# Attention heads of a fused two-layer kernel: the division moved ahead of a round's first marking, and each exponential placed two slots behind its turned scores

## The reference, cut to what matters

```
qr, kr = apply_rope(q, cos, sin), apply_rope(k, cos, sin)
draft = einsum('bhqd,bhkd->bhqk', qr, kr) + causal(neg)
_, draft_indices = top_k(draft, 128)
mask = full(neg); mask[draft_indices] = 0; mask = causal(neg)
attn = softmax(draft / 4 + mask)
out = einsum('bhqk,bhkd->bhqd', attn, v) @ Wo.T
```

## Time and profile before

| | |
|---|---|
| median of the runs | 3397.38 us |
| the profiled execution | 3398.37 us |
| its span | 3396.6 us |
| TensorE matmul, busy | 3019.7 us (89%) |
| VectorE, busy | 2404.0 us (71%) |
| ScalarE, busy | 1961.9 us (58%) |
| GpSimd, busy | 1532.1 us (45%) |
| attention heads, from the first sample to the last division | 2115.5 to 3256.2 us |

### The profile page before, as it was taken

The page is one execution under the profiler, slowest core; times in us unless marked ns, Lnnn a source line. Parts: engine busy times, 40 slices in busy tenths (PEclk is TensorE's granted clock), DMA queues, the critical chain, the costliest instruction groups (busy, mean ns, idle before and its releaser), DMA issues. The chain is left out here.

```text
span 3396.6 us, 49801 instructions
## 1 busy us (share of the span) xinstructions
PE 3019.7 (89%) x15644; PEld 1834.0 (54%) x15737; DVE 2404.0 (71%) x4659; ACT 1961.9 (58%) x4170; POOL 1532.1 (45%) x3508
## 2 busy tenths in 40 slices
PE   7999999999999999999999877487888788888779
PEld 4455454554554645545445435266666666666654
DVE  5677696786876967769679428587777777777640
ACT  1464564545545635456455115788888888888621
POOL 2245263362442633625426200766666666666410
PEclk9999999999999999999999988577777777777889
DMA  2222132231322322313212010000000000000010
GB/s 83 62 84 84 70 116 81 69 106 68 97 72 79 115 74 81 91 71 106 87 53 97 13 45 1 1 1 1 1 2 1 2 2 1 1 2 1 1 48 25
DMA packets 65800, 169.58 MB, mean 50 GB/s; under 512 B 11776, under 2 KB 19328, under 8 KB 64512
## 3 DMA queue, kind: packets, MB, share of 16 engines
q1 hardware_dynamic: 54448, 115.17, 10.5%
q10 hardware_dynamic: 11088, 51.19, 4.3%
HBM read 161.08 MB, written 5.24 MB: 49 GB/s over the span
## 5 line engine op out<-in xcount | busy, mean ns | idle before, releaser
L1898 ACT ACTIVATE X<-ah_z,ah_trial 128x256 bf16<-128x256 f32 (+6 forms) x896 | 732.4, 824 | 25.0 <-POOL ah_trial L2001 13.9
L1082 ACT ACTIVATE m_mix<-m_mix,m_cs 128x128 f32<-128x128 f32 x1024 | 312.9, 388 | 257.2 <-DMA m_mix<-cs_rows 257.2
L1853 PE MATMUL ah_ps_o<-a_v,X 128*128 128x17 f32 x2304 | 353.3, 282 | 44.8 <-DVE hT L2098 44.8
L1853 PEld LDWEIGHTS ah_ps_o<-a_v,X 128*128 128x128 f32 x2304 | 337.9, 220 | 52.1 <-ACT X L1909 49.7
L1909 ACT ACTIVATE X<-ah_ps_e 128x512 f32<-128x512 f32 (+3 forms) x384 | 185.8, 485 | 191.5 <-PE ah_ps_e L1840 128.5
L2070 DVE TENSOR_SCALAR_CACHE_REDUCE X<-ah_z,ah_cut 128x256 bf16<-128x256 f32 (+6 forms) x224 | 193.6, 875 | 128.7 <-POOL ah_cut L2006 128.7
L964 POOL TENSOR_TENSOR m_xdec<-m_xdt,m_decay_out 128x512 f32<-128x512 f32 x112 | 142.8, 1275 | 213.1 <-DVE m_xdt L1208 202.0
L887 PE MATMUL m_ps_x<-m_w_out,m_gate 128*128 128x512 f32 x512 | 234.1, 600 | 0.0
L887 PE MATMUL m_ps_d<-m_w_out,m_gate 128*128 128x512 f32 x512 | 233.5, 599 | 0.0
L2083 DVE MAX8 ah_top<-ah_ps_m 128x8 f32<-128x256 f32 (+6 forms) x224 | 185.9, 830 | 67.0 <-PE ah_ps_m L1803 58.8
L992 POOL TENSOR_TENSOR m_squares<-m_squares 128x256 f32<-128x256 f32 x128 | 104.1, 813 | 276.9 <-ACT m_squares L1094 276.9
(11 more groups left out here) (297 smaller groups left out, 7518.9 us busy)
## 6 DMA issues: line engine op xcount, KB each, us to landing
m_mix<-cs_rows SPq DMA_DIRECT2D x128, 512.0 KB, 4.5
m_w_proj<-in_w_proj ACTq DMA_DIRECT2D x69, 512.0 KB, 3.3
m_fade<-fade_rows SPq DMA_DIRECT2D x224, 128.0 KB, 3.0
m_w_out<-in_w_out ACTq DMA_DIRECT2D x7, 2048.0 KB, 7.7
X<-in_x SPq DMA_DIRECT2D x8, 256.0 KB, 5.0
m_w_out<-in_w_out SPq DMA_DIRECT2D x1, 2048.0 KB, 10.6
x_away<-X SPq DMA_DIRECT2D x1, 2048.0 KB, 10.9
X<-x_away SPq DMA_DIRECT2D x8, 256.0 KB, 7.3
```

What stands on the lines that cost most here:

```text
L1082: act.activation(mix[:, u % 3, h, :], mix[:, u % 3, h, :], ACT.Relu, bias=cs[:, c, h0 + h:h0 + h + 1], scale=-1.0).then_inc(lag_done, 1)
L1853: last = pe.matmul(ps_o[:, t, :], eT[:, g % 3, b * P:(b + 1) * P], v[:, b0 + b, h // REP, :], start=i == 0 and b == 0, stop=b0 + b == t, s ...
L1898: act.activation(sign[:, at % 2, 0:(t + 1) * P], z[:, h % RING, cols(t)], ACT.Sign, bias=trial[:, h % RING, 0, t - 1:t], scale=-1.0, accum ...
```

## The change

Two edits, both inside `attention_heads_fast`. `LATER` goes from 1 to 2, so slot `i` of ScalarE's round now holds chunk `i-2` of head n-3: slots 0 and 1 hold the last two chunks of head n-4, and slots 2 to 11 the first ten of head n-3. And VectorE's `divide(n - 4)` moves from behind pick 1, evacuation 1 and take 3 to a place ahead of take 1. TensorE's and GpSimd's lists stay as they are.

```
-    LATER = 1
+    LATER = 2
...
                     add_sample(n + 1)
+                if live(n - 4):
+                    divide(n - 4)
                 if live(n - 2):
                     take(n - 2, 1)
                     take(n - 2, 2)
...
-                    if t == 1 and live(n - 4):
-                        divide(n - 4)
```

## The result

The changed kernel takes 3390.3 us (median of 15 executions, fastest 3385.4), the kernel before 3396.3 on the same chips. The ratio is 0.998 [0.9972, 0.9988]: a real gain, of some 6 us and not of 38. One of the fifteen executions took 11779 us, with a mean granted clock of 0.57, and is left out of the ratio. The profiled execution took 3390.3 us with a span of 3388.5, which is 8.1 less than that of the profiled execution before. This is the rival "the two edits cancel", which I had given 14%.

A forecast was written before the change was run, and what follows sets the result against it. A ring of waits, no engine, bounds the kernel. Period 26.2 + 6.8 = 33.0 us, 1.12 less than 34.12, over 26 periods 29 us; 29 - 0.5 + 10 = 38, from 3398.4 to 3360 us, range 3318 to 3392.

The forecast's parts named there:

- the two edits cancel: Rival, 14%: late chunk 11 holds the division, which holds the marking; period stays 34.0 to 34.2 us, total say 3392.
- The ring: Chain of waits in the heads: marking, turned scores, exponential, last count, cut, next marking; 34.12 us a period.
- two new gates: Row copy waits for the twelfth chunk, 0.5 to 2 us; division, ahead of marking, waits for chunk 11's addition, some 3.
- The division moved: VectorE's division ahead of the first marking: TensorE's marked scores of tile 2 start 1.7 us earlier after it.
- The exponentials moved: ScalarE's exponentials get a slot of slack, on average 2.4 us; its 190 us of waits for turned scores largely go.
- X: Stretch from VectorE's first marking to the end of the twelfth chunk of turned scores: 26.2 us, between 25.05 and 26.9.
- the tail: Chain from ScalarE's row copy through chunk 11's exponential, its addition and the division to the next marking: 6.8 us, 6.2 to 7.4.
- three signs: Wrong if marking still waits for cut, twelfth chunk ends later than 27.3 us, or row copy to marking outside 6.2 to 7.4.
- Theory A: Links of the ring add up; making any link shorter or longer moves the period by as much.
- Theory B: Clock falls in step with rounds hold the period, 34.1 us; TensorE at another clock level offsets a changed link.
- The last rounds: Final periods of the heads, without new scores, less work on ScalarE: together about 10 us gained, between 4 and 13.
- The slower rival: Rival, 15%: low clock spreads to TensorE's stretch from chunk 8 to chunk 11; period 36.4 us, total 3450, milder 3423.

The follow-up runs named there:

- the pads: Changed kernel plus an unused VectorE reduction between division and first marking of each head: 384 columns (about 0.5 us), 3391.4 us; 1024 columns (1.2 us), 3403.9 us.
- 0.5 us of pad: Unused 384-column VectorE reduction between division and first marking: on the changed kernel 3391.4 us; on the version with chunks 10 and 11 in slot 0, 3342.0 us.
- the late row copy: Changed kernel with ScalarE's second row copy of a round two counts later, in the next round: 3324.9 us, ratio 0.9792.
- the long pad: Changed kernel plus an unused VectorE reduction over 1024 columns between division and first marking of each head: 3403.9 us, ratio 1.0028.

## Why the prediction was wrong

**The ring and the two new gates were right.** The marking gave up its wait for the cut, the reciprocal waits for the added values (5.00 us, where I had some 3), TensorE's wait for the division went to 0.2 us, its pause ahead of chunk 1 is 1.39 us (over 1 predicted), and the row copy waits 1.71 us (0.5 to 2). The marked scores of tile 2 stand 2.82 us behind the marking (2.9). ScalarE's waits for turned scores were missed: 135.5 us, not 60 to 90.

**The division moved** was right in place and price, 1.7 us; done alone it brought 1.71 us a period.

**The exponentials moved** was wrong in the sum. X and the tail were taken from mixed rounds, 26.2 and 6.8, and each came at the end of its range: 26.77 and 7.25. The two misses, 0.57 + 0.45, and 0.10 for a link that the sum left out make up the 1.12 us that I had expected to gain. The step that failed is the choice of a middle value for each of these two terms, as if they were independent. They are not: with the pads the tail grew from 7.26 to 8.38 us and X fell from 26.89 to 25.74. In the changed kernel the clock is at half where the round begins, through the adding of chunk 11 in the tail and the first 6 us of X. My own sentence on the upper tail, 7.4, gave 33.6 with X unchanged. None of the three signs by which I would have called the prediction wrong came up: the marking no longer waits for the cut, and a tail of 7.25 and a twelfth chunk at 26.77 lie inside their limits, so limits for single terms did not guard the sum.

**The rival that came true** had 14% because I took its cause for a coincidence of two sizes. Its cause as I wrote it is shown, that the late chunk 11 holds the division and the division the marking: the division alone brings 53 us, and with chunk 11 back at slot 0 both edits bring 97. That the two sizes match so well seems to be no coincidence either. The mean period stayed within 0.05 us of 34.13 in five kernels whose links differ by up to 1.1 us (before, after, the exponentials alone in its profiled execution, pads of 0.5 and 1.2 us), and at 30.72 in two more. Away from such a value the cost comes in a jump: 0.5 us of pad leaves 34.13 as it is, but makes 31.9 of 30.72. With the pads, what changed in TensorE was its busy time and granted clock, with the same instructions. Theory A, on which the whole sum stood, falls for changes of a microsecond; the period of before was no baseline from which 1.12 us could be taken. That the clock's falls are what holds the period is what fits the rows; no run here set the clock by itself, and filling the pauses brought only 14 us, so that part is not shown, nor why it is just 34.13 and 30.72. Theory B as I wrote it is not the whole either: it had 34.1 with the division alone, where the period was 32.41, and missed with slot 0 and with the late row copy. Where a link changed by much, the period did move: by 1.7 us for the 1.7 of the division, and by 3.4 for the 2.4 of the tail. The last is again no plain sum.

The Trainium skill, page "TensorE: Matmul & The Clock Gate", section "A second HAM failure mode: psum-queue depth-cycling", has short pauses swing the clock between its levels. The trace agrees in part. The fall in the middle of the changed kernel's round, between 2552.0 and 2552.5, comes right behind a pause of 1.45 us. The fall at its end comes as the pause of 1.39 us begins, and with that pause filled the clock fell all the same, amid matmuls.

**The last rounds** were predicted at 10 us (4 to 13) and gave 7.9. Of the start's 0.5 us, 0.33 came (2232.83 for 2232.50). One count of mine was off: of the 26 periods before, 15 are of the long kind and 11 of the short. Nothing in the sum hangs on it.

**The slower rival** asked for half clock from chunk 8 to chunk 11. That stretch, 2559.20 to 2566.40, is at 1.00: it did not happen.

## What to carry to other kernels

Two edits that each shorten a ring can cancel: before one gives slack to a producer, look at what reads its last product, for here an exponential two slots later held the division, and the division the next marking. Measure each alone, since one part may carry the gain and the other take it (3343.5 us for the division alone, 3390.3 together), and a single item put back in its place, chunk 11, can be worth more than both. Where a round repeats and the granted clock falls at the same points in every round, do not take middle values for the stretches, and ask what a small pad does before trusting that a microsecond saved is a microsecond won. When a pad costs something, look where: most of what the long one cost stood in a stretch that had no pad.

## What the hardware showed unexpectedly

A steady period can be insensitive to the work in it. A link on the path that was 1.14 us longer left 34.14 us a round, with the clock of TensorE going from 0.75 to 0.80 and its busy time from 29.08 to 27.27 us for the same 224 instructions. TensorE can work 24 us without a pause and stay at half clock: with the long pad it did, behind the last marking, where the changed kernel has 1.00 for the same work. The same kernel can also take either of two times: the exponentials alone took 3391.9 us in one execution and 3412 to 3417 in four. And more matmuls made a kernel faster: eight of 512 columns in each round, 14 us less.
